# Norm turns two tiles behind their roots, key sums and low parts on GpSimd

## What is computed

```python
x = x + 0.5 * ffn(layernorm(x))
x = x + attn(layernorm(x))
x = x + 0.5 * ffn(layernorm(x))

def attn(x):            # x is (2, 1024, 512)
    q, k, v = x @ Wq.T, x @ Wk.T, x @ Wv.T      # 16 query heads, 4 key and value heads of 32
    q = q * cos + rotate_half(q) * sin          # rotate_half: [-x2, x1] of the two halves
    k = k * cos + rotate_half(k) * sin
    scores = einsum(q, repeat(k, 4)) * 32 ** -0.5
    return einsum(softmax(scores), repeat(v, 4)) @ Wo.T

def ffn(x):             # shared experts: width 704; 8 experts of width 352, the best two of a token
    y = (silu(x @ sw1) * (x @ sw3)) @ sw2
    return y + sum(weight[e] * ((silu(x @ rw1[e]) * (x @ rw3[e])) @ rw2[e]) for e in top2)
```

## Time and profile before

| | us |
|---|---|
| median of 3 runs | 1826.81 |
| lowest and highest run | 1823.87, 1834.07 |
| profiled execution | 1813.59 |
| its span, first to last instruction | 1811.8 |

### The profile page before, as it was taken

How to read it: one execution, slowest core, us unless ns; L and a number is a source line. 1 busy time by engine, 2 the same in 40 slices (tenths; PEclk the granted TensorE clock), 3 DMA queues, 4 the chain that set the end, 5 groups by cost and what they waited for, 6 DMA issues and landing times.

```text
span 1811.8 us, 25089 instructions
## 1 busy us (share of the span) xinstructions
PE 1685.2 (93%) x8596; PEld 1342.8 (74%) x8596; DVE 1081.7 (60%) x1846; ACT 857.9 (47%) x1274; POOL 977.0 (54%) x727
## 2 busy tenths in 40 slices
PE   6999999999977989999999999887799999999997
PEld 5888899898866756666666666545688889999885
DVE  4554322222587879999999999995445432222226
ACT  4322232222224358989898988872333122322220
POOL 3115673336522148989898989840030619550646
PEclk9999999999988989999999999998989999999998
DMA  9205543333640000000000000003010535432427
GB/s 341 87 25 217 207 175 131 120 132 114 192 140 1 1 2 1 1 1 1 1 1 2 1 1 2 12 13 142 1 52 1 223 121 194 161 140 85 166 83 243
DMA packets 54310, 160.01 MB, mean 88 GB/s; under 512 B 6704, under 2 KB 7600, under 8 KB 51632
## 3 DMA queue, kind: packets, MB, share of 16 engines
q1 hardware_dynamic: 41360, 84.74, 13.4%
q0 software_dynamic: 12832, 73.67, 11.5%
HBM read 102.29 MB, written 55.84 MB: 87 GB/s over the span
## 4 chain that ended last, share of the span: by engine, by line
PE 58%; DVE 18%; issue 8%; ACT 7%; DMA 7%; POOL 0%; SPq 0%; ACTq 0%; DVEq 0%; POOLq 0%
PE PS L1050 10%; PE PS L1052 9%; PE PS L1051 9%; DVE nmf L1831 5%; DVE Ph L1848 4%; PE PS L1246 4%; DMA xn<-x_routed 3%; ACT Ph L1526 3%; ACT PT L1519 2%; DMA xs<-x_routed 2%; PE PS L1279 2%; PE PS L1172 2%; PE PS L1280 2%; PE PS L1177 2%; PE PS L1175 2%
## 5 line engine op out<-in xcount | busy, mean ns | idle before, releaser
L1988 POOL TENSOR_TENSOR Pl<-PT,Ph 128x1024 fp32r<-128x1024 f32 x176 | 435.9, 2491 | 81.6 <-ACT Ph L1526 76.4
L1831 DVE TENSOR_REDUCE nmf<-PS 128x1 f32<-128x1024 f32 x256 | 307.7, 1213 | 29.0 <-PE PS L1246 26.7
L1519 ACT ACTIVATE PT<-PS 128x1024 f32<-128x1024 f32 x256 | 258.7, 1015 | 19.9 <-DVE Pl L1854 11.7
L1279 PE MATMUL PS<-Ph,V 128*65 128x512 f32 x512 | 206.5, 403 | 11.9 <-DVE Pl L1854 10.9
L1280 PE MATMUL PS<-Pl,V 128*65 128x512 f32 x512 | 201.9, 394 | 0.0
L1526 ACT ACTIVATE Ph<-PT 128x1024 fp32r<-128x1024 f32 x184 | 194.1, 1055 | 1.5
L1903 POOL TENSOR_TENSOR W<-raw,W 128x544 fp32r<-128x544 f32 x144 | 190.1, 1354 | 1.5
L1806 DVE TENSOR_TENSOR thid<-thid,PS 128x352 f32<-128x352 f32 x78 | 40.6, 521 | 245.8 <-ACT thid L1445 245.8
L1246 PE MATMUL PS<-KS,QS 96*128 96x512 f32 x512 | 170.8, 415 | 16.9 <-ACT PT L1519 11.3
L1264 PE MATMUL PS<-QS,KS 98*128 98x512 f32 x512 | 174.8, 423 | 6.0 <-DVE nmf L1831 5.8
L1445 ACT ACTIVATE thid<-PS 128x352 f32<-128x352 f32 x78 | 36.2, 464 | 260.4 <-PE PS L1177 260.4
(11 more groups left out here) (183 smaller groups left out, 4111.9 us busy)
## 6 DMA issues: line engine op xcount, KB each, us to landing
raw<-ffn_w POOLq DMA_DIRECT2D x18, 2176.0 KB, 10.3
y_routed<-ytile SPq DMA_DIRECT2D x78, 256.0 KB, 2.0
xn<-x_routed SPq DMA_DIRECT2D x40, 256.0 KB, 2.9
x_routed<-xq SPq DMA_DIRECT2D x1, 9984.0 KB, 28.7
xs<-x_routed SPq DMA_DIRECT2D x38, 256.0 KB, 3.6
raw<-ffn_w SPq DMA_DIRECT2D x6, 768.0 KB, 10.4
raw<-ffn_w SPq DMA_DIRECT2D x2, 2176.0 KB, 9.1
x_home<-X SPq DMA_DIRECT2D x4, 1024.0 KB, 5.7
```

The costliest lines, as they stand in the source:

```text
L1279: e.matmul(PS[0:VCOL, ob, :], V[:, b * QT + kt, g, :], high_part(u)[:, js], start=kt == 0, stop=False)
L1519: e.activation(PT[:, u % PTBUF, :], PS[:, i:i + 2, :].rearrange("p b n -> p (b n)"), ACT.Exp, scale=SCALE).then_inc(p_ready.sem, 1)
L1831: e.tensor_reduce(nmf[:, (n % 3) * REP + h, t:t + 1], PS[:, i:i + 2, :].rearrange("p b n -> p (b n)"), AX.X, ALU.max, negate=True).then_in ...
L1988: e.tensor_tensor(low_part(u)[:], PT[:, u % PTBUF, :], high_part(u)[:], ALU.subtract).then_inc(pl_pool.sem, 1)
```

## The change

1. The list beside the output projection is written out by hand: statistics of a group, then the roots one to two output tiles later, then the norm turns two output tiles behind the roots, so that a norm turn and the head turns around it use different banks. The first two `shared_split` items move into the stage.
2. The key sum, the keys' low part and the low part of all stacks move from DVE to POOL. The first two groups' stacks get their own buffer (`early_TS`), for which ACT waits for `home_out` of group 3.
3. The two products of the changed halves become one, with the halves read in reversed order.
4. The pending combines and norm pieces of the first projected tiles are spread otherwise: one combine in a slot, the last norm's pieces later, its last two after the eighth tile.
5. The maxima of the first two heads are placed before the last row maximum.

```diff
-    beside = [norms[other][3]]
-    beside += [norms[other][4], norms[other][5]]
     work.extend(("gather", 0, t) for t in group_tiles(LATE))
-    beside += [norms[other][6] + sums[LATE][0] + sums[LATE][1], sums[LATE][2] + sums[LATE][3] + norms[third][0]]
-    beside += [norms[third][1] + norms[third][2], norms[LATE][0]]
-    beside += [norms[third][3] + norms[LATE][1], norms[third][4]]
-    beside += [norms[third][5], norms[third][6] + norms[LATE][2]]
-    beside += [norms[LATE][3], norms[LATE][4]]
-    beside += [norms[LATE][5] + norms[LATE][6]]
+    beside = [norms[other][3],
+              norms[other][4], norms[other][5],
+              norms[other][6] + sums[LATE][0], sums[LATE][1] + norms[third][0],
+              sums[LATE][2], sums[LATE][3] + norms[third][1] + norms[third][2],
+              [], norms[LATE][0],
+              norms[third][3], norms[third][4],
+              norms[third][5] + norms[LATE][1], norms[third][6] + norms[LATE][2],
+              norms[LATE][3], norms[LATE][4],
+              norms[LATE][5] + norms[LATE][6]]
...
             work.append(("project", t, h + 1))
+            if i == NT - 1 and h == REP - 2:
+                for h2 in range(2):
+                    work.extend([("place_max", 0, h2), ("place_low", 0, h2)])
...
-    for h in range(REP):
+    for h in range(2, REP):
         work.extend([("place_max", 0, h), ("place_low", 0, h)])
...
+    first, other = ([[item] for item in norm_pieces(2, g)] for g in ORDER[:2])
+    load = [("shared_in", 1, i) for i in range(3)]
+    beside = {3: load, 4: first[0], 5: first[1] + first[2], 7: first[3], 8: first[4] + other[0], 9: first[5] + other[1],
+              10: first[6], 11: other[2], 12: other[3] + [("shared_split", 1, 0)], 13: other[4],
+              14: other[5] + [("shared_split", 1, 1)], 15: other[6]}
     turned = [t for g in ORDER for t in group_tiles(g)]
     for i in range(NT + 2):
         if i < NT:
             work.append(("turn_heads", turned[i]))
         if i >= 2:
-            tt = turned[i - 2]
-            work.append(("project_out", tt))
-            if beside and beside[0][0][3] == 0:
-                work.extend(beside.pop(0))
-            if beside:
-                work.extend(beside.pop(0))
...
+            work.append(("project_out", turned[i - 2]))
+            work.extend(beside.get(i - 2, []))
...
+    early_TS, at = place("early_TS", (P, 2, REP, STK), F32, at)
...
+                if not beside_heads(n):
+
+                    act.wait_ge(home_out[ORDER[1]])
...
-            e.tensor_tensor(turned[:, h0:h1, 0:HALF], qk[:, :, HALF:], sin[:, :, 0:HALF], ALU.mult)
-            e.tensor_tensor(turned[:, h0:h1, HALF:], qk[:, :, 0:HALF], sin[:, :, HALF:], ALU.mult)
+            halves = "p h (c d) -> p h c d"
+            e.tensor_tensor(turned[:, h0:h1, :].rearrange(halves, d=HALF), qk.rearrange(halves, d=HALF)[:, :, ::-1, :],
+                            sin.rearrange(halves, d=HALF), ALU.mult)
...
-                dve.step(rotary(t, PS[:, bq + 1, :], NH, NQK, kv_done))
+                rotary(t, PS[:, bq + 1, :], NH, NQK, kv_done).then_inc(k_products.sem, 1)
                 e.tensor_tensor(V[:, t, :, HD + 1:], v, V[:, t, :, 0:HD], ALU.subtract).then_inc(v_lo.sem, 1)
-                dve.after_step()
-                e.tensor_tensor(qka[:, i, NH:, :], qka[:, i, NH:, :], turned_halves(t)[:, NH:, :],
-                                ALU.add).then_inc(k_rotated.sem, 1)
...
-            elif kind == "split_keys":
-                t, = key
-                dve.wait_ge(k_hi, t)
...
+                if piece == 1:
+                    pool.wait_ge(k_products, t)
+                    e.tensor_tensor(qka[:, i, NH:, :], qka[:, i, NH:, :], turned_halves(t)[:, NH:, :],
+                                    ALU.add).then_inc(k_rotated.sem, 1)
...
+                pool.wait_ge(stack_hi, n, t)
+                src = qtok[:, b * QT + t, g * REP * HD:(g + 1) * REP * HD].rearrange("p (h d) -> p h d", d=HD)
+                e.tensor_tensor(stack_of(n, t)[:, :, HD:2 * HD].bitcast(F32R), src, stack_of(n, t)[:, :, 0:HD],
+                                ALU.subtract).then_inc(stack_lo.sem, 1)
+            elif kind == "split_keys":
+                t, = key
+                pool.wait_ge(k_hi, t)
```

More of the change, by code:

```diff
@@ L451, in order_of_work @@
     work.append(("attention_end",))
-    beside = []
+    first, other = ([[item] for item in norm_pieces(2, g)] for g in ORDER[:2])
[3 more added lines that the diff above has]
+              14: other[5] + [("shared_split", 1, 1)], 15: other[6]}
     turned = [t for g in ORDER for t in group_tiles(g)]
@@ L457, in order_of_work @@
         if i >= 2:
-            tt = turned[i - 2]
-            work.append(("project_out", tt))
-            if beside and beside[0][0][3] == 0:
-                work.extend(beside.pop(0))
-            if beside:
-                work.extend(beside.pop(0))
-            if tt % TPG == TPG - 1:
-                g = tt // TPG
-                if g == ORDER[0]:
-                    work.extend(("shared_in", 1, i) for i in range(3))
-                if g in ORDER[:2]:
-                    beside.extend(norm_slots(2, g))
-    work.extend(item for slot in beside for item in slot)
+            work.append(("project_out", turned[i - 2]))
+            work.extend(beside.get(i - 2, []))
     work.extend(("shared_in", 1, i) for i in range(3, len(SHARED_PIECES)))
-    work.extend(("shared_split", 1, i) for i in (0, 1))
     work.extend(item for slot in ffn(1, [slot for g in (LATE, *FIRST) for slot in combined(1, g)]) for item in slot)
@@ L661, in macaron @@
     v_ones, k_ones = signal("v_ones"), signal("k_ones")
-    kv_done, v_hi, v_lo, k_rotated, k_hi, k_lo, k_turned, k_ready = (
-        signal(n) for n in ("kv_done", "v_hi", "v_lo", "k_rotated", "k_hi", "k_lo", "k_turned", "k_ready"))
+    kv_done, v_hi, v_lo, k_products, k_rotated, k_hi, k_lo, k_turned, k_ready = (
+        signal(n) for n in ("kv_done", "v_hi", "v_lo", "k_products", "k_rotated", "k_hi", "k_lo", "k_turned", "k_ready"))
     q_done, q_rotated, q_ready = signal("q_done"), signal("q_rotated"), signal("q_ready")
-    stack_hi, stack_lo, stack_lo_pool, stack_turned, stack_ready = (
-        signal(n) for n in ("stack_hi", "stack_lo", "stack_lo_pool", "stack_turned", "stack_ready"))
+    stack_hi, stack_lo, stack_turned, stack_ready = (
+        signal(n) for n in ("stack_hi", "stack_lo", "stack_turned", "stack_ready"))
     max_done, max_taken, max_turned, max_hi, max_ready = (
@@ L806, in macaron @@
             t, piece = key
-            for a in ((), (kv_done, v_hi, v_lo, k_rotated, k_hi), (), (q_done, q_rotated, q_ready))[piece]:
+            for a in ((), (kv_done, v_hi, v_lo, k_products, k_rotated, k_hi), (), (q_done, q_rotated, q_ready))[piece]:
                 a.plan(t)
@@ L814, in macaron @@
         elif kind == "stack":
-            for a in (stack_hi, stack_lo_pool if beside_heads(key[0]) else stack_lo):
+            for a in (stack_hi, stack_lo):
                 a.plan(*key)
@@ L899, in is_projected_after, with stack_of @@
         return PROJECTED.index(t) >= n
+    def stack_of(n, t):
+        return (TS if beside_heads(n) else early_TS)[:, stack_place[n, t] % 2]
     def high_part(u):
@@ L1743, in project @@
                 dve.wait_ge(v_hi, t)
-                dve.step(rotary(t, PS[:, bq + 1, :], NH, NQK, kv_done))
+                rotary(t, PS[:, bq + 1, :], NH, NQK, kv_done).then_inc(k_products.sem, 1)
                 e.tensor_tensor(V[:, t, :, HD + 1:], v, V[:, t, :, 0:HD], ALU.subtract).then_inc(v_lo.sem, 1)
-                dve.after_step()
-                e.tensor_tensor(qka[:, i, NH:, :], qka[:, i, NH:, :], turned_halves(t)[:, NH:, :],
-                                ALU.add).then_inc(k_rotated.sem, 1)
             elif piece == 3:
                 rotary(t, PS[:, bq, :], 0, NH, q_done).then_inc(q_rotated.sem, 1)
-        def stack(n, t):
-            b, g = KV_GROUPS[n]
-            place_ = stack_place[n, t]
-            i, tile = place_ % 2, b * QT + t
-            src = qtok[:, tile, g * REP * HD:(g + 1) * REP * HD].rearrange("p (h d) -> p h d", d=HD)
-            dve.wait_ge(stack_hi, n, t)
-            e.tensor_tensor(TS[:, i, :, HD:2 * HD].bitcast(F32R), src, TS[:, i, :, 0:HD],
-                            ALU.subtract).then_inc(stack_lo.sem, 1)
         def store_head(n, h, hf):
@@ L1819, in vector_program @@
                 project(*key)
-            elif kind == "split_keys":
-                t, = key
-                dve.wait_ge(k_hi, t)
-                e.tensor_tensor(kst[:, t % 2, :, 2 * HD:].bitcast(F32R), qka[:, t % 2, NH:, :],
-                                kst[:, t % 2, :, 0:HD], ALU.subtract).then_inc(k_lo.sem, 1)
-            elif kind == "stack" and not beside_heads(key[0]):
-                stack(*key)
             elif kind == "row_max":
```

17 lines of the change are left out of this document (6 added, 11 removed).

## The result

| | before | after |
|---|---|---|
| median of 4 runs, us | 1827.0 | 1807.62 |
| lowest and highest run | 1823.87, 1834.07 | 1804.29, 1810.50 |
| profiled execution, its span | 1813.59, 1811.8 | 1810.50, 1808.7 |
| mean granted clock | 0.973 | 0.970 |

The ratio of after to before is 0.9888, 95% interval 0.9855 to 0.9921: by it 20.5 us of 1827 are saved, by the medians 19.4; the forecast was 20.2. The agreement of the sum hides deviations of single stages that partly cancel, so I read both traces by stages, from starts of PE's rows. "First half" runs from the first product with `Wqkv` to the first row maximum, "second half" on to the last such product, "placing" from there to the first score, "output stage" from the first head turn to the first product of the second feed-forward part, "shared part" from there to the first turn of a routed hidden tile.

The account below looks back on a forecast made before the run. PE was taken as the bound, winnable only where it waits or runs at the lower clock. The terms -21 - 0.5 + 2.5 - 1.2 = -20.2 us took the median 1826.8 to 1807, range 1796 to 1819 (own range 1802 to 1813).

Parts of the forecast that it names:

- Part 1: Output projection: reordered norms remove PE's waits and lower clock; -21.9 us worked out, -21 taken.
- Part 2: Projection: low parts and key sums on POOL relieve DVE, half kept in the first half; -0.5 us, in the second half.
- Part 3: Projection: new order of combines and norms in the first half, POOL queue waits included; net +2.5 us, ends 0 and +8.
- (a): First half of projection: first tile's key sum stands behind POOL's last gathers; PE idles 4.4 us.
- DVE has caught up: First half of projection: despite later roots, DVE does the queries of tile 11 at 554, before at 553.8.
- A third fall of the clock: First half of projection: another spell of lower clock, counted only in the upper end of +8 us.
- (b): Ninth projected tile: key sum stands behind POOL's fill of ones, +3.0 us, covered by the late norm turns' +3.8 wait.
- Part 4: Placing of maxima before scores: first two placed early, scores start sooner, PE stalling 1.7 us inside; -1.2 us.
- The turned product: Projection: one product over reversed halves takes 0.60 us, against 0.34 + 0.33 for two.
- the upper end: Projection: the reversed product takes 1.2 us, as a 1024-element row, costing +4.5 us over 8 tiles.
- (1): Projection loses more: POOL queue waits and late norm turns add up, +8 to +12 instead of +2.5; 1814, chance 0.15.
- (2) to (5): Projection gains, 1796, 0.12; output stage half, 1816, 0.06; reversed product slow, 1847, 0.03; norm turns still wait, 1828, 0.02.

Follow-up runs that it names:

- rest_only: The changed kernel with the old list beside the output projection; 1813.91 us, ratio 1.0006 to the kernel before.
- old_list: The changed kernel with the old list of pieces beside the first eight projected tiles; 1795.88 us, ratio 0.9905 to the kernel before.
- first_sum_dve: The changed kernel with only the first projected tile's key sum back on DVE; 1786.08 us, ratio 0.9865 to the kernel before.
- after_again: The changed kernel, unaltered, run and profiled again beside the others; 1793.15 us, ratio 0.9895 to the kernel before.
- out_near: The kernel before with the new output list, but norm turns one output tile behind their roots instead of two; 1798.2 us, one run.
- keysum_dve: The changed kernel with all key sums back on DVE, low parts staying on POOL; 1788.95 us, ratio 0.9872 to the kernel before.

## Why the prediction was right, and where not

**The number.** 1807 was forecast and 1807.6 measured. So close a hit is luck. Against the forecast's terms the output stage gave 1 us more, the first half cost 2 us more and the second 0.7 more, and the runs of one session spread over 6 to 10 us.

**What bounds the kernel.** Right: PE's waits in the output stage and the lower clock behind them were 22 us.

**Part 1, -21.** Measured -22.3 and -21.8. Each step of the working stands: end at 39.1 us behind the sixth head turn (39.2), first norm wait 0.87 (1.0), no loss of clock, splits hidden. The -21.9 worked out was better than the -21 that I took for safety.

**Part 2, low parts on POOL.** The step's time was 0.46 (taken 0.39, bound 0.91). Half of DVE's relief was taken as kept: right in kind, as far as single profiles show: the first half is 1.5 us shorter with the low parts on POOL (65.49 against 67.02), 1.9 with only the keys' (65.15). DVE's waiting beside POOL shows in after's rows:

```profile
538.87 1.32 POOL L1955 TENSOR_TENSOR qtok<-qka,early_qkr 128x512 f32<-128x512 f32 x1 [3.71 <-DVE qka L1740]
539.30 1.44 DVE L1716 SCALAR_TENSOR_TENSOR X<-late_pairs,pair_w,X 128x512 f32<-128x512 f32 x1
...
548.46 1.75 POOL L1955 TENSOR_TENSOR qtok<-qka,early_qkr 128x512 f32<-128x512 f32 x1 [5.00 <-DVE qka L1740]
549.08 1.68 DVE L1719 SCALAR_TENSOR_TENSOR X<-late_pairs,pair_w,X 128x512 f32<-128x512 f32 x1
```

At 539.30 the combine starts beside POOL's sum and ends 0.55 us behind it. At 548.46 POOL is second, 0.16 us behind a combine, takes 1.75 instead of 1.3, and the next combine waits in turn. The Trainium skill (SBUF — State Buffer, Who interferes with whom) says just this: a DVE instruction with two SBUF inputs and a GpSimd one that reads SBUF exclude each other, and whichever starts second waits. The rows agree. The second half was forecast at -0.5: the product gave 0.4, but POOL's low parts took 0.6 or more (which of them was not separated), and it is +0.1 to +0.2. That term had the wrong sign, by 0.7 us.

**Part 3, +2.5: the term that was too small.** The wait of (a) came where it was said, with 3.49, 4.45, 5.07 (rest_only) and 4.38 us (old_list) for 4.4; the terms of its sum as written add up to 526.5, though, not to 526.8. The walk through DVE's queue held too. Counted from the first projected product, DVE's roots are 5.3 us later than in before (forecast 7), the queries of tile 11 start at 36.2 us (before 37.6, forecast 37.8), and the last product of the eight tiles ends at 63.5 (before 64.9, forecast 62.5 to 64.9). So "DVE has caught up" was right, as a comparison with before.

What the sum had too small stands behind that product. From there the first stack's turn comes 4.4 us later than in before, where 3.8 were forecast. Then the clock is at its lower level (0.50), and from that turn to the first row maximum are 3.88 us instead of 2.44: 1.4 us for which the sum had nothing. "A third fall of the clock" stood only at its end of +8. Measured -1.4 + 4.4 + 1.4 = +4.5 (+4.6 in the second pair of profiles), where the forecast had -1.3 + 3.8 = +2.5.

The forecast had the first key sum's place on POOL only inside this walk, without a price of its own for the whole half. It is 5.3 us or more, as first_sum_dve shows: 4.1 from the order of the queues, the other 1.2 by DVE's longer wait for matmuls at the lower clock. DVE's backlog did not absorb it. DVE's low part waits 5.12 us for ACT, in order, with the whole backlog behind it. Without this, the first half is 66.3 against 67.2 and 68.0 in before, a gain of 0.9 to 1.7 for the rest of the change.

I had put the later wait at the second norm turn; it was at the key bank, one step earlier, since ACT's copy of the keys stands behind normalizations that wait for roots. ACT's queue was not walked there.

**(b) and its cover.** Right both ways: no wait for the ninth key sum in after, where the late norm turns stand ahead of it, and 2.83 us in old_list; the second half there is 2.5 longer than with the key sums on DVE. Forecast 3.0.

**Part 4, -1.2.** Measured -1.2; PE's stall inside it 1.46 (1.7).

**The turned product.** 0.68 for 128x512, starting 0.60 ahead of the next instruction, as taken; the upper end is refuted. Two signals that I had named as decisive, a first half within 62 to 74 us and a product under 0.8, stand.

**The median.** I carried over the 13.2 us between before's profile and its median. Medians then differ by 19.4, the forecast being 20.2. But after's own profile, forecast at 1793.4, read 1810.5: 10 us were the stall; 3.2 lie ahead of the projection and 2.6 behind the shared part, in stages with the same instructions; the projection has 2.7 more than forecast, and the output stage 1.3 less. Why the first session's runs of before lie 12 to 16 us above its medians in the others (1827.0 against 1811 to 1814.5) stays open; after's lie 14 above after_again's.

**Rivals.** (1) was the nearest: (a) and the late norm turns did each bring a spell of lower clock, only (b) was covered, and it came to +4.5 and +4.6 instead of +8 to +12. (2) to (5) fell.

## What to carry to other kernels

Before an operation is moved to an engine with free time, look at what stands ahead of its first instance in that engine's queue; the mean load says nothing of it. Follow the chain of a stall before you count on another engine's backlog to hide it: where that engine is a link of the chain, the stall came through whole. Price a piece of work that is put off to the end of a stage with the waits and the clock that it finds there: the new list of the projection gained 5.3 us before the last product and lost 5.9 behind it. Compare busy time at each clock level, not only idle time, since the idle time of before and after was equal. In a stage where turned tiles share PSUM banks, both the distance to the producer and the bank have to be kept apart; giving up one of them cost 7 to 10 of the 22 us.

## What the hardware showed

**The clock after short waits.** Behind waits of 2.72 and 4.08 us the granted clock was 0.50. Behind 2.13 in out_near it stayed at 1.00, but in after, behind a wait of 2.02, it was 0.60 (timeline of PE, then the window behind the wait), and in keysum_dve, behind 1.89, it was 0.59 from 566.05 to 568.00:

```profile
575.68 0.92 PE L1058 MATMUL PS<-identf,xn 128*128 128x128 f32 x4 [2.02 <-DVE xl L1552]
```

```profile
575.68:580.00 4.32, 4.32 (x22) 4.26 (x23) 2.17 (x6) 2.53 (x5) 1.31 (x1) 0.60 0.00 0
```

So the bound that I took from one row (1.97 kept the clock) is none: between 1.9 and 2.1 us both outcomes occur, and the length of the last wait alone does not tell them apart.

**A stall without a semaphore.** In after's first profile PE waits for its own issue between 1406 and 1418, in pieces of up to 1.0 us. ACT's next instruction comes after 17.38 us, where its like come after 3 to 4 in after_again; the view names no engine of this core for it. Timeline of PE and ACT, then the window of the stretch:

```profile
1408.97 0.40 PE L1053 MATMUL PS<-xh,W 128*128 128x512 f32 x1 [0.89 <-issue]
...
1418.90 0.60 ACT L1436 ACTIVATE hid<-PS 128x512 f32<-128x512 f32 x1 [17.38 <-remote]
```

```profile
1405.00:1423.00 18.00, 11.93 (x31) 7.11 (x30) 3.37 (x6) 1.23 (x2) 8.61 (x10) 0.72 0.38 145
```

It cost 10 to 11 us in one of fourteen profiled executions; the other thirteen have 169.6 to 172.9 us for the shared part. POOL issues its scatters in these microseconds, but it does so in after_again too, without a stall, so the cause stays open. From one profile it would have been read as a cost of the change.
